# GpSimd's scatters and sends in two expert layers: 16 sends spread over 24 blocks, scatters falling behind and catching up

## The reference, cut to what matters

```python
x = x + attn_a(layernorm(x), ...)        # linear attention, x is 8 x 512 x 128, float32
x = x + ffn(layernorm(x), Wr, W1, W2)    # expert layer 1
x = x + attn_b(layernorm(x), ...)        # delta-rule memory
x = x + ffn(layernorm(x), Wr, W1, W2)    # expert layer 2, same weights

def ffn(h, Wr, W1, W2):                  # 8 experts, 128 -> 512 -> 128
    g = softmax(h @ Wr); top2_w, top2_idx = top_k(g, 2)
    top2_w = top2_w / sum(top2_w)
    expert_out[e] = relu(h @ W1[e]) @ W2[e]
    return sum over the two chosen experts of expert_out * weight
```

## Time and profile before

| | |
|---|---|
| median of 3 runs | 1086.84 us (1085.21 to 1088.23) |
| profiled execution | 1078.89 us |
| its span, first to last instruction | 1077.2 us |
| mean granted TensorE clock | 0.956 of full speed |
| PE busy | 957.5 us (89%) |
| VectorE busy | 542.7 us (50%) |
| ACT busy | 539.7 us (50%) |
| GpSimd busy | 370.9 us (34%) |
| layer 1, scatter of block 0 to scatter of block 70 | 306.4 to 467.0 us |
| layer 2, the same | 876.5 to 1054.7 us |

### The profile page before, as it was taken

How to read it: one execution, slowest core, us unless ns; L and a number is a source line. 1 busy time by engine, 2 the same in 40 slices (tenths; PEclk the granted TensorE clock), 3 DMA queues, 4 the chain that set the end, 5 groups by cost and what they waited for, 6 DMA issues and landing times.

```text
span 1077.2 us, 31428 instructions
## 1 busy us (share of the span) xinstructions
PE 957.5 (89%) x11919; PEld 717.0 (67%) x11919; DVE 542.7 (50%) x1912; ACT 539.7 (50%) x1082; POOL 370.9 (34%) x387
## 2 busy tenths in 40 slices
PE   7999999999998789969998899998888888778990
PEld 6455666566798789955544855674475787768990
DVE  4236445543764222136678477659758774340104
ACT  2443433433143355537666756755684644435760
POOL 2200332223235555541220121223313356555551
PEclk9999999999999899989999899999999899978995
DMA  8733431334022322141111201110145031213206
GB/s 215 196 80 80 101 82 34 90 95 100 21 73 63 82 73 65 43 122 40 41 41 42 82 1 44 48 48 19 52 151 149 22 79 50 61 55 86 77 32 236
DMA packets 83506, 82.75 MB, mean 77 GB/s; under 512 B 12335, under 2 KB 64388, under 8 KB 82848
## 3 DMA queue, kind: packets, MB, share of 16 engines
q1 hardware_dynamic: 68864, 58.30, 20.9%
q0 software_dynamic: 10176, 19.04, 5.6%
q10 hardware_dynamic: 4320, 3.41, 1.1%
HBM read 53.96 MB, written 27.64 MB: 76 GB/s over the span
## 4 chain that ended last, share of the span: by engine, by line
PE 73%; DVE 11%; ACT 5%; issue 5%; DMA 2%; another core or an unknown queue 2%; POOL 1%; SPq 0%; ACTq 0%; POOLq 0%; DVEq 0%
PE b_ring L1734 7%; PE b_ring L1279 6%; PE a_ring L1279 6%; PE b_ring L1290 6%; PE a_wide L1290 6%; PE a_ring L820 5%; PE a_ring L824 5%; PE a_wide L838 5%; PE a_y L879 4%; PE b_g L1781 4%; PE b_g L1756 4%; PE b_ring L1796 3%; DVE b_kq L2141 2%; ACT early L1901 2%
## 5 line engine op out<-in xcount | busy, mean ns | idle before, releaser
L1734 PE MATMUL b_ring<-b_hT,b_qkT 128*128 128x512 f32 x256 | 121.1, 609 | 5.2 <-DVE b_kq L2141 4.8
L2141 DVE SCALAR_TENSOR_TENSOR b_kq<-b_exp,b_ring 128x512 f32<-128x512 f32 x128 | 83.0, 683 | 41.6 <-ACT b_exp L1887 40.0
L276 POOL DMA_INDIRECT expert_rows<-f_route_sent,f_route_place_id x64 | 62.2, 972 | 98.8 <-DVE f_route_place_id L232 50.8
L1290 PE MATMUL b_ring<-wide,b_v 128*128 x568 | 82.0, 291 | 14.5 <-ACT b_v L1305 13.0
L1279 PE MATMUL b_ring<-b_v,b_kq 128*128 128x128 f32 x568 | 82.1, 291 | 11.7 <-ACT b_v L1300 8.8
L1887 ACT ACTIVATE b_exp<-b_ring 128x512 f32<-128x512 f32 x128 | 73.5, 604 | 32.3 <-PE b_ring L1734 20.4
L1290 PE MATMUL a_wide<-wide,phiqT 128*128 x568 | 78.9, 284 | 11.4 <-issue 7.8
L1734 PEld LDWEIGHTS b_ring<-b_hT,b_qkT 128*128 128x128 f32 x256 | 45.1, 189 | 61.8 <-issue 39.8
L1290 PEld LDWEIGHTS b_ring<-wide,b_v 128*128 128x128 f32 x568 | 74.9, 205 | 16.0 <-issue 15.8
L1279 PEld LDWEIGHTS b_ring<-b_v,b_kq 128*128 128x128 f32 x568 | 75.1, 206 | 14.2 <-ACT b_v L1300 10.2
L1256 POOL DMA_INDIRECT expert_parts<-phiqT,a_rn_wide x59 | 62.4, 1058 | 58.1 <-ACT phiqT L1320 32.6
(11 more groups left out here) (332 smaller groups left out, 1857.2 us busy)
## 6 DMA issues: line engine op xcount, KB each, us to landing
a_rn_wide<-norm_compact SPq DMA_DIRECT2D x28, 512.0 KB, 10.5
wide<-in_L_ffn_W SPq DMA_DIRECT2D x32, 256.0 KB, 5.6
a_rn_wide<-expert_rows SPq DMA_DIRECT2D x71, 65.0 KB
b_coef<-gram_compact SPq DMA_DIRECT2D x4, 1024.0 KB, 4.9
early<-expert_parts SPq DMA_DIRECT2D x16, 256.0 KB, 5.0
b_hT<-expert_rows SPq DMA_DIRECT2D x56, 65.0 KB
x<-in_L_attn_a_x SPq DMA_DIRECT2D x8, 256.0 KB, 4.3
early<-expert_parts SPq DMA_DIRECT2D x4, 512.0 KB, 5.8
```

Of the source, the lines that this page charges most:

```text
L276: pool.indirect_dma_start(self.rows, bass.IndirectOffsetOnAxis(self.place_id[:, k, n:n + 1], 0), self.sent[:, n, k, :], None).then_inc(sel ...
L1290: ins = pe.matmul(self.y_bank[j % 2][:, 0:P], self.hidT[:, b % HID_SLOTS, f, :], self.C["w2"][:, bass.ds(e, 1), f, :].rearrange("p a c -> ...
L1734: pe.matmul(ring[n % 4][:, :], w, hT[:, g % 2, half * 512:half * 512 + 512], start=True, stop=True)\
L2141: dve.scalar_tensor_tensor(out=kq[:, p % 2, half:half + FOURS // 2, slot:slot + T * FOUR], in0=exps[:, n % EXPS, :].rearrange("p (a n) -> ...
```

## The change

A helper `begun(pool, j)` is new: GpSimd waits until hidden block j is done.

Layer 1: the scatters of blocks 0 to 9 stay. Then eight groups of three blocks follow, each with two scatters and two sends and a wait for each of the three blocks. After the last group, at block 34, 26 scatters are issued. The remaining 45 have a wait each, spread evenly over blocks 34 to 70.

Layer 2: over two blocks there are two sends and one scatter. Steps 4, 5, 6 and 7 start at blocks 0, 10, 18 and 26; between steps 4 and 5 there are three scatters. At block 34, 19 scatters are issued. The remaining 52 are spread evenly over blocks 34 to 70. On PE, ACT and VectorE the parts of step 6 come one or two blocks sooner and those of step 7 three blocks sooner, and the parts of the block tables move with them.

```diff
@@ layer 1, GpSimd
-            for j in range(BLOCKS):
+            SENDS_AT, SPAN = 10, 24
+            AFTER = SENDS_AT + 4 * NT
+            for j in range(SENDS_AT):
                 ffn.scatter(pool, j)
                 if j == 1:
                     router.root(pool, LAST)
-                for r, first in ((LAST - 1, 10), (LAST, 18)):
-                    if first <= j < first + 2 * NT:
-                        route_slot(r)
-                        router.send_one(pool, r, j - first)
+            for c in range(4 * NT // 2):
+                r, i, b = LAST - 1 + c // NT, 2 * (c % NT), SENDS_AT + 3 * c
+                ffn.begun(pool, b)
+                ffn.scatter(pool, SENDS_AT + 2 * c)
+                route_slot(r)
+                router.send_one(pool, r, i)
+                ffn.begun(pool, b + 1)
+                ffn.scatter(pool, SENDS_AT + 2 * c + 1)
+                ffn.begun(pool, b + 2)
+                router.send_one(pool, r, i + 1)
+            for j in range(AFTER, BLOCKS):
+                ffn.begun(pool, SENDS_AT + SPAN + (j - AFTER) * (BLOCKS - SENDS_AT - SPAN) // (BLOCKS - AFTER))
+                ffn.scatter(pool, j)
@@ class ExpertLayer
+    def begun(self, pool, j):
+
+        wait_apart(pool, self.F["hid_done"], self.first + j + 1, self.K.passed)
@@ layer 2, GpSimd
-            for i in range(2 * NT):
-                if i == 2:
+            for c in range(NT):
+                if c:
+                    ffn.begun(pool, 2 * c)
+                router.send_one(pool, route(4), 2 * c)
+                if c == 0:
                     root(5)
-                elif i == 4:
+                elif c == 1:
                     ln_out.root(pool, C["minus_half"], 3)
-                if i:
-                    wait_apart(pool, ffn.F["hid_done"], ffn.first + i, K.passed)
-                router.send_one(pool, route(4), i)
-                if i >= 3:
-                    ffn.scatter(pool, i - 3)
-            for j in range(2 * NT - 3, BLOCKS):
+                ffn.begun(pool, 2 * c + 1)
+                router.send_one(pool, route(4), 2 * c + 1)
+                ffn.scatter(pool, c)
+                if c == 3:
+                    root(6)
+            j = NT
+            for r, b, between in ((5, 10, 3), (6, 18, 0), (7, 26, 0)):
+                for k in range(between):
+                    ffn.begun(pool, b - 2 + k * 2 // 3)
+                    ffn.scatter(pool, j + k)
+                j += between
+                for c in range(NT):
+                    ffn.begun(pool, b + 2 * c)
+                    router.send_one(pool, route(r), 2 * c)
+                    ffn.scatter(pool, j + c)
+                    ffn.begun(pool, b + 2 * c + 1)
+                    router.send_one(pool, route(r), 2 * c + 1)
+                    if r == 5 and c == 1:
+                        root(7)
+                j += NT
+            for j in range(j, BLOCKS):
+                ffn.begun(pool, 34 + (j - 19) * 37 // 52)
                 ffn.scatter(pool, j)
-                if j == 6:
-                    root(6)
-                elif j == 11:
-                    root(7)
-                for r, first in ((5, 7), (6, 16), (7, 24)):
-                    if first <= j < first + 2 * NT:
-                        router.send_one(pool, route(r), j - first)
@@ layer 2, PE
-                for r, at in ((5, (2, 3, 7)), (6, (11, 12, 15)), (7, (20, 21, 24))):
+                for r, at in ((5, (2, 3, 7)), (6, (10, 11, 14)), (7, (17, 18, 21))):
@@ layer 2, ACT
-                if j + W1_AHEAD in B_FULL:
-                    act.wait_ge(block_table.table_ready, 2 + B_FULL.index(j + W1_AHEAD))
+                if j + W1_AHEAD - 1 in B_FULL:
+                    act.wait_ge(block_table.table_ready, 2 + B_FULL.index(j + W1_AHEAD - 1))
...
-                for r, at in ((5, (2, 6)), (6, (11, 14)), (7, (20, 23))):
+                for r, at in ((5, (2, 6)), (6, (10, 13)), (7, (17, 20))):
@@ layer 2, VectorE
-                elif j in (11, 12):
-                    block_table.part(dve, 1, j - 11)
-                elif j == 13:
+                elif j == 11:
+                    block_table.part(dve, 1, 0)
+                elif j == 12:
                     choose(6)
-                elif j in (14, 16):
-                    block_table.part(dve, 1, 2 + (j - 14) // 2)
+                elif j in (13, 14):
+                    block_table.part(dve, 1, j - 12)
+                elif j == 15:
+                    place(6)
+                elif j == 16:
+                    route_normalize(7)
                 elif j == 17:
-                    place(6)
-                elif j == 18:
-                    route_normalize(7)
+                    block_table.part(dve, 1, 3)
+                elif j == 19:
+                    choose(7)
                 elif j == 22:
-                    choose(7)
-                elif j == 25:
                     place(7)
-                elif 26 <= j < 26 + BlockTable.PARTS:
-                    block_table.part(dve, 2, j - 26)
+                elif 23 <= j < 23 + BlockTable.PARTS:
+                    block_table.part(dve, 2, j - 23)
```

## The result

The changed kernel takes 1083.61 us (median of 14 runs, 1079.78 to 1088.77) beside 1088.74 us for the kernel before in as many runs: ratio 0.9957, 95% interval 0.9939 to 0.9976. It is faster by 5 us, where 20 were forecast. The profiled execution has a span of 1085.1 us, longer than the 1077.2 of before: the profiled execution of before (1078.89 us) is shorter than all 14 of its runs, the one of after (1086.86 us) is above its median, and 8 us lie between the two expert layers, where no code differs. So I compare layers, from the first relu to the last, as ACT's timeline has them.

What follows compares the result with a forecast made beforehand. First half of each layer held by signals coming late while GpSimd issues indirect DMAs without pause, second half bound by TensorE. Savings of 10.7 + 9.4 = 20 us off the 1086.84 us median gave 1067 us, range 1040 to 1089.

Steps and rivals of the forecast that it cites:

- forecast's own 1057 to 1077: Whole kernel: range of the main case, 20 us saved to 1067 us, chance 0.54.
- The reading of the stalls: First halves of both layers: other engines' signals come late while GpSimd issues indirect DMAs without pause; 61 us to win.
- Rival C: First halves: strings are not cut, since waits are long met; what is won is given back, about 1084 us; chance 0.12.
- E: Both layers: VectorE's copies are the cause, stalls stay, catch-up takes 76 us for 70; 6 us slower, 1093 us; chance 0.04.
- Rival B: Both layers: short strings are nearly free; layer 1 saves 18.7, layer 2 saves 28.9, giving 1039 us; chance 0.18.
- The send stretches: First halves: loss left of 8.8 us in layer 1 (1.1 per four-string), 17 in layer 2 (1.0 per block pair).
- its 2 us: First halves: sign that the prediction is right, PE idles of at most 2 us there.
- The catching up: Second halves: doubled scatters cost 8 x 0.3 = 2.4 us in layer 1, 15 x 0.6 = 9 us in layer 2.
- Rival D: Layer 2, blocks 34 to 70: scatter debt paid where PE was full; 11.5 us slower, 1098 us; chance 0.12.
- The block slots: Layer 2, block 38: PE waits once for its late fetch, 2.5 us, plus 1 us for lower clock.
- Routing three blocks sooner, cost 0: Layer 2, steps 6 and 7 on PE, ACT, VectorE: same instructions in another block, 0, with 2 us allowed either way.
- The rule weighed: GpSimd can't write descriptors during VectorE's 2-port SBUF copies; trace shows 0.19 us each; by it alone stalls would stay.

Runs made afterwards that it cites:

- threes_no_waits: Against the kernel before: layer 1 scatters three at a time from block 40; layer 2 GpSimd's changed order without waits on hidden blocks. 1.0209, where the kernel before takes 1088 us.
- defer: Kernel before with only GpSimd's order of layer 2 changed; PE, ACT, VectorE and layer 1 as before. 1.0019, where the kernel before takes 1088 us.
- sooner: Kernel before with only layer 2's routing steps 6, 7 and tables sooner; GpSimd still sends and scatters by turns. 1.0022, where the kernel before takes 1088 us.
- defer_again: Kernel before with only GpSimd's order of layer 2 changed, run again where the kernel before takes 1026 us: 0.9864, from two runs.
- l2_only: Kernel before with the whole changed layer 2 on all engines, layer 1 as before: 0.9904, where the kernel before takes 1026 us.
- l1_only: Kernel before with GpSimd's changed order in layer 1 alone, layer 2 as before: 0.9993, where the kernel before takes 1026 us.

## Why the prediction was wrong

The way of the change was right, and the time, 1083.61 us, lies inside the range of 1040 to 1089 but outside the forecast's own 1057 to 1077. The gain was a quarter of the forecast.

*The reading of the stalls: right on the slow kind, as far as it ties idles to strings.* `threes_no_waits` shows it from both sides: strings made longer give longer idles, with nothing else changed in layer 1 and only the waits gone against `defer` in layer 2. That it is the engines' signals that come late was argued and isn't shown. Rivals C and E are out: the strings were cut, and the first halves did gain. Rival C's time, 1084 us, was hit all the same, by another way. Rival B is out by the loss behind block 34.

*The send stretches: right.* Layer 1 was to keep 8.8 of 21.9 us of loss, so to save 13.1; it saved 12.3. Layer 2 was to save 21.9; it saved 18.4. The 1.1 us per string of four and 1.0 per pair of blocks were about right: 9.6 us stayed in layer 1 for 8.8, and 20.5 in layer 2 for 17. One sign of the prediction was missed: three PE idles of the first halves, 2.24, 3.79 and 3.85 us, are over its 2 us.

*The catching up: this step failed.* "8 x 0.3 = 2.4 us" for layer 1 measured 8.6. "15 x 0.6 = 9 us" with 3.5 for the slots in layer 2 measured 19.9. Of that, 3.2 us are the two waits for fetches (one was forecast, at 2.5 and 1 more), so 16.7 stand where 9 were put. Together 28.5 us where I had 14.9. These 13.6 us, with 4.3 from the send stretches, bring the forecast's 20.1 us down to the 2.3 that the two profiles differ by, and they are most of the 15 us by which the forecast missed the medians. The 0.3 came from two strings near 430 us of the kernel before, behind which PE's timeline has no idle of 0.15 us or more. A three of `threes_no_waits` costs some 0.7 us. That more than doubles the term and still doesn't fill it: six strings of three or more in layer 1's catch-up would be 4 us. The changed kernel pays some 1.4 us for each of these six, and 1.4 again for each of the twelve in layer 2's. In layer 1 five of the six PE idles end with a late relu; in the test the first four end with a late copy of the transposed block, at 0.44 to 0.62 us, and four more with a relu, at 0.16 to 1.29. So it may matter where in a block a string falls. The changed kernel also differs from the test in that scatters lag and are held by a wait on a hidden block. Which of these makes the rest stays open.

*Rival D was half right.* Its mechanism, the debt paid where PE was full, is what ate the gain, with 28.5 us against a saving of 30.7. Its size was not reached: it needed 28 us in layer 2, or 0.76 per block, and layer 2's catching up took 16.7, or 0.45 per block, without the waits for fetches. I gave it 0.12 because one scatter a block cost nothing there; that says nothing of three in a string.

*The block slots: right in place.* The forecast wait is there, at block 38, with 1.35 us for 2.5. A second one, 1.87 us at block 40, wasn't forecast ("40 and on just hold"). The fetch of block 40 goes at 980.30, 3.06 us behind SP's last write of filler rows at 977.24, an item of SP's queue that the prediction left out; whether SP waited for that write or for a scatter isn't told by the rows.

*Routing three blocks sooner, cost 0: right for the slow kind* (`sooner` 1.0022, and its interval of 0.9989 to 1.0054 includes 1). On the quick kind `defer_again` has the layer's full gain without it, so there it does nothing measurable either.

*The rule weighed* decided nothing: the send stretch was won though VectorE's copies stayed. The Trainium skill (SBUF — State Buffer, the box on the "DVE blocks DMA" trap) describes a copy that holds up GpSimd; these idles are the reverse, GpSimd's DMAs holding up the others.

*What the prediction didn't have:* on the quick kind the change gains 1.2%, by a way not among my rivals. A full GpSimd sent the last rows late, and blocks 24 and 40 waited for them. In the trace of before the blocks went so slowly that sends came in time, so this wait couldn't be seen in it; it could have been worked out from 1.28 us per DMA and a block at 1.90.

## What to carry to other kernels

Spreading work on an engine that is full at one time moves its load to a time when others are full. Price the time in which the debt is paid with the same measured price as the time that is relieved, not with the mildest example in the trace. When an engine's queue is full, ask which of its items somebody waits for: putting off the scatters that nobody needed yet was worth 1.2% on the quick kind, where strings cost nothing.

## What the runs showed of the hardware

On the slow kind, indirect DMAs issued by GpSimd 0.30 us apart hold up the other engines' progress: a string of three costs some 0.7 us, and one of 21 kept ACT idle for 14.49 us, until 3 us after its end. On the quick kind 49 in a string cost nothing (PE busy 63.00 of 63.00 us beside it), and the same kernel takes 1026 instead of 1088 us; in the profiles 48.3 us of the difference lie in the two expert layers (layer 1 as in `l2_only`, layer 2 as in `l1_only`). GpSimd's own time for a send has the same median on both, 0.96 us in layer 1. The change gains 0.4% and, measured again, 0.2% (interval up to 1.0009) on the slow kind, and 1.2% on the quick one.
